# The start-up of a two-block attention kernel: how batch 0's rows arrive, what warms TensorE, and who normalises and rounds the rows

## The reference, cut to what matters

```
x = L0_attn_hidden_states                 # (2, 512, 256) f32: 2 batches of 512 tokens
xn = layernorm(x)                         # over the 256 features, eps 1e-5
s = attention0(xn, Wq, Wk, Wv, Wo)        # 16 heads, 4 key/value heads, head size 16
g = silu(ffn0(xn, w_gate_up, w_down))     # 256 -> 2 x 1024 -> 256
x = x + s * g
...                                       # second block: linear attention and
                                          # a mixture of 8 experts, top 1
```

## The kernel before, in words

Two places of the program that the steps below speak of:

```
            for b in range(B):
                dve.wait_ge(x_in_s[b], 16)
                norm_sums(TB * b, TB * b + TB)
                for stage in range(4):
                    norm_root(b, stage)
                apply_norm(0, b)
...
    fill[KD:5 * KD] = [*up0, *fill[2 * KD:3 * KD], *gate2, *fill[3 * KD:4 * KD]]
    early(KD)


    stacks = [("stack_T", 0, c) for c in STACK_ORDER]
    plan += stacks[:3]
```

## Time and profile before

| | us |
|---|---|
| median of three runs (lowest, highest) | 345.54 (345.40, 347.27) |
| the profiled execution | 345.08 |
| its span, first to last instruction | 343.3 |
| PE busy | 315.3 (92%) |
| DVE busy | 228.9 (67%) |
| ACT busy | 158.7 (46%) |
| POOL busy | 61.5 (18%) |

### The profile page before, as it was taken

The page is one execution under the profiler, slowest core; times in us unless marked ns, Lnnn a source line. Parts: engine busy times, 40 slices in busy tenths (PEclk is TensorE's granted clock), DMA queues, the critical chain, the costliest instruction groups (busy, mean ns, idle before and its releaser), DMA issues.

```text
span 343.3 us, 4810 instructions
## 1 busy us (share of the span) xinstructions
PE 315.3 (92%) x1602; PEld 186.8 (54%) x1602; DVE 228.9 (67%) x494; ACT 158.7 (46%) x289; POOL 61.5 (18%) x80
## 2 busy tenths in 40 slices
PE   2977989999999999999999999999989999999940
PEld 2645565454465454465545456556655676666630
DVE  3997848778475676877976763039898575446940
ACT  1476514575776655554474465523315622232310
POOL 5007750000010000000000002100503421033063
PEclk9999989999999999999999999999999999999995
DMA  7900019028091370400000006108934993038410
GB/s 250 406 6 2 0 49 201 1 61 191 1 207 45 83 169 1 124 0 3 1 1 3 0 1 207 41 2 326 361 95 118 392 428 140 30 124 258 165 53 20
DMA packets 19483, 39.19 MB, mean 114 GB/s; under 512 B 1826, under 2 KB 15363, under 8 KB 18176
## 3 DMA queue, kind: packets, MB, share of 16 engines
q1 hardware_dynamic: 17904, 35.69, 32.6%
q0 software_dynamic: 1552, 3.15, 2.6%
HBM read 34.54 MB, written 15.22 MB: 145 GB/s over the span
## 4 chain that ended last, share of the span: by engine, by line
PE 78%; DVE 15%; issue 3%; ACT 1%; DMA 1%; POOL 1%; DVEq 0%; POOLq 0%; ACTq 0%
PE ps L1728 12%; PE ps L1673 9%; PE ps L1641 8%; PE ps L1741 8%; PE ps L1663 7%; PE ps L1783 6%; PE ps L1799 6%; PE ps L1811 6%; PE ps L1546 3%; DVE nmax L1222 3%; PE ps L1580 2%; PE ps L1848 2%; PE ps L1525 2%; PE ps L1773 1%; DMA x<-in_x 1%
## 5 line engine op out<-in xcount | busy, mean ns | idle before, releaser
L1222 DVE TENSOR_REDUCE nmax<-ps 128x1 f32<-128x512 f32 x128 | 85.5, 687 | 35.0 <-PE ps L1641 34.3
L957 ACT ACTIVATE shared<-ps 128x512 f32<-128x512 f32 x128 | 74.1, 594 | 53.6 <-PE ps L1663 52.7
L1641 PE MATMUL ps<-experts 96*128 96x512 bf16 x128 | 48.2, 384 | 1.6 <-DVE experts L1229 1.1
L1663 PE MATMUL ps<-experts 99*128 99x512 bf16 x128 | 48.3, 382 | 0.0
L1741 PE MATMUL ps<-shared,experts 128*128 128x256 f32 x128 | 37.5, 386 | 0.0
L1673 PE MATMUL ps<-shared,experts 128*32 128x512 f32 x256 | 34.1, 605 | 0.3 <-ACT shared L957 0.3
L1641 PEld LDWEIGHTS ps<-experts 96*128 96x128 bf16 x128 | 12.5, 98 | 36.7 <-DVE nmax L1222 18.3
L1741 PEld LDWEIGHTS ps<-shared,experts 128*128 128x128 f32 x128 | 23.4, 190 | 8.9 <-issue 2.5
L965 ACT ACTIVATE experts<-ps 96x1024 bf16<-96x1024 bf16 x18 | 17.9, 1018 | 11.6 <-PE ps L1580 11.6
L1546 PE MATMUL ps<-late_weights,xnT 128*128 128x512 f32 (+1 forms) x64 | 22.5, 492 | 0.3 <-DVE shared L1134 0.3
L1783 PE MATMUL ps<-experts,shared 128*128 x88 | 20.9, 380 | 0.8 <-ACT shared L1032 0.8
(11 more groups left out here) (232 smaller groups left out, 516.9 us busy)
## 6 DMA issues: line engine op xcount, KB each, us to landing
experts<-in_experts SPq DMA_DIRECT2D x8, 1536.0 KB, 11.3
slot_rows<-in_empty SPq DMA_DIRECT2D x4, 2080.0 KB, 12.2
shared<-in_wgu SPq DMA_DIRECT2D x1, 2048.0 KB, 10.9
x<-in_x SPq DMA_DIRECT2D x2, 512.0 KB, 5.5
shared<-in_wdn SPq DMA_DIRECT2D x1, 1024.0 KB, 12.8
expert_results<-in_empty SPq DMA_DIRECT2D x1, 1024.0 KB, 6.9
token_rows<-x SPq DMA_DIRECT2D x1, 1024.0 KB, 16.0
token_rows<-gx SPq DMA_DIRECT2D x1, 1024.0 KB, 4.5
```

The source lines that it names most:

```text
L957: nc.scalar.activation(probs[:, n % 2, hh, :], ps[:, 2 + hh % 2, :], ACT.Exp, scale=float(HD) ** -0.5).then_inc(s["exp_done"], 1)
L1222: nc.vector.tensor_reduce(nmax[:, 4 * t + hh:4 * t + hh + 1], ps[:, m % 2, :], AX, ALU.max, negate=True).then_inc(s["max_done"], 1)
L1641: nc.tensor.matmul(ps[:, m % 2, :], qs[0:KS, b, GR * g + hh, P * t:P * t + P], ks[0:KS, b, g, :], start=True, stop=True).then_inc(s["score ...
L1663: nc.tensor.matmul(ps[:, 2 + hh % 2, :], ks[0:KM, b, g, P * t:P * t + P], qs[0:KM, b, GR * g + hh, :], start=True, stop=True).then_inc(s[" ...
```

## The change

- SP loads batch 0's rows in four transfers of 128 KB, each with a semaphore of its own, and DVE waits tile by tile in `norm_sums`. All later loads are issued behind them.
- DVE first writes 0.5 into a 128x128 part of `tanh_g` (`halves_ready`). PE starts its warm-up on that tile: 22 f32 products instead of 18 transposes, and it waits for the constants only afterwards.
- DVE normalises tiles 0 and 1 of batch 0, ACT tiles 2 and 3 (`half_norm`). The counts of `rows_norm` are adapted to that.
- ACT does `projections(0)` ahead of `round_rows(0, k)`.
- DVE computes `x_low` of batch 0 behind `prepare(0)` instead of ahead of it.
- In `plan` the first two gate pieces stand behind the first three stacks instead of ahead of them.

```diff
-WARM_UP = 18
+WARM_UP = 22
...
     fill[KD:5 * KD] = [*up0, *fill[2 * KD:3 * KD], *gate2, *fill[3 * KD:4 * KD]]
-    early(KD)
-
-
     stacks = [("stack_T", 0, c) for c in STACK_ORDER]
     plan += stacks[:3]
+    early(KD)
...
-            sp.dma_start(x[:, 0:TB, :], x_in[:, 0:TB, :]).then_inc(x_in_s[0], 16)
+            for j in range(TB):
+                sp.dma_start(x[:, j, :], x_in[:, j, :]).then_inc(x_in_s[j], 16)
             sp.dma_start(cst[:, 0:early_c], const_in[:, 0:early_c]).then_inc(s["const_loaded"], 16)
             sp.dma_start(wqkv, wqkv_in).then_inc(s["wqkv_loaded"], 16)
-            sp.dma_start(x[:, TB:NT, :], x_in[:, TB:NT, :]).then_inc(x_in_s[1], 16)
+            sp.dma_start(x[:, TB:NT, :], x_in[:, TB:NT, :]).then_inc(x_in_s[TB], 16)
...
             nc.scalar.activation(identb[:], ident, ACT.Copy).then_inc(s["identb_ready"], 1)
+            act.wait_ge(s["std_ready"], 1)
+            for j in range(TB // 2, TB):
+                nc.scalar.activation(xn[:, j, 0:D], x[:, j, :], ACT.Identity, scale=st1[:, 4, j:j + 1], bias=st1[:, 5, j:j + 1]
+                                     ).then_inc(s["half_norm"], 1)
...
             round_weights(0)
             round_weights(1)
+            projections(0)
             for k in range(KD):
                 round_rows(0, k)
-            projections(0)
...
-            def norm_sums(j0, j1):
+            def norm_sums(j0, j1, first=False):
 
                 for j in range(j0, j1):
+                    if first:
+                        dve.wait_ge(x_in_s[min(j, TB)], 16)
                     last = nc.vector.bn_stats(bn[:, j, :], x[:, j, :])
...
+            nc.vector.memset(tanh_g[:, 0, 0:P], 0.5).then_inc(s["halves_ready"], 1)
             for b in range(B):
-                dve.wait_ge(x_in_s[b], 16)
-                norm_sums(TB * b, TB * b + TB)
+                norm_sums(TB * b, TB * b + TB, first=True)
                 for stage in range(4):
                     norm_root(b, stage)
-                apply_norm(0, b)
+                apply_norm(0, b, TB if b else TB // 2)
...
-            dve.wait_ge(s["qkv_psum"], TB)
-            for k in range(KD):
-                dve.wait_ge(s["x_high_ready"], k + 1)
-                nc.vector.tensor_tensor(x_low(0, k), xnT[:, k, 0:S], x_high(0, k).bitcast(F32), ALU.subtract).then_inc(s["x_low_ready"], 1)
...
             nc.vector.tensor_copy(place_in_stack(5, 0, HEADS), place_in_stack(1, 0, HEADS)).then_inc(s["slots_copied"], 1)
+            dve.wait_ge(s["qkv_psum"], TB)
+            for k in range(KD):
+                dve.wait_ge(s["x_high_ready"], k + 1)
+                nc.vector.tensor_tensor(x_low(0, k), xnT[:, k, 0:S], x_high(0, k).bitcast(F32), ALU.subtract).then_inc(s["x_low_ready"], 1)
...
-            pe.wait_ge(s["const_loaded"], 16)
 
-            keep_warm(WARM_UP, 7)
+            pe.wait_ge(s["halves_ready"], 1)
+            for _ in range(WARM_UP):
+                nc.tensor.matmul(ps[:, 7, 0:P], tanh_g[:, 0, 0:P], tanh_g[:, 0, 0:P], start=True, stop=True)
+            pe.wait_ge(s["const_loaded"], 16)
             for b in range(B):
                 for t in range(TB):
-                    pe.wait_ge(s["rows_norm"], TB * b + t + 1)
+                    if b == 0 and t >= TB // 2:
+                        pe.wait_ge(s["half_norm"], t + 1 - TB // 2)
+                    else:
+                        pe.wait_ge(s["rows_norm"], t + 1 + TB // 2 * b)
```

More of the change, by code:

```diff
@@ L505, in two_gated_blocks @@
         miscb = misc.bitcast(BF16)
-        x_in_s = [sem(f"x_loaded{b}") for b in range(B)]
+        x_in_s = [sem(f"x_loaded{n}") for n in range(TB + 1)]
         names = ("raw_T raw_ready router_mean router_centred logits_scaled gates_ready acol_psum acol_ready act_step attn_T_ready bias_added branch_free branch_psum branch_ready "
-                 "const_loaded cos1 counts down_ready down_tanh dve_step e_down e_gate e_gated e_h e_tanh e_up "
+                 "const_loaded halves_ready half_norm cos1 counts down_ready down_tanh dve_step e_down e_gate e_gated e_h e_tanh e_up "
                  "early_gate_free early_up_free end_free exp_done experts_here first_part gate_free gate_ready heads_T "
@@ L803, in scatter @@
                 pool.wait_ge(s["slots_emptied"], 16 * EMPTYINGS)
-                pool.wait_ge(s["rows_norm"], NT + TB * (b + 1))
+                pool.wait_ge(s["rows_norm"], NT - TB // 2 + TB * (b + 1))
                 for j in range(TB * b, TB * b + TB):
@@ L1584, in _ @@
                     bank = place(it)[0]
-                    pe.wait_ge(s["rows_norm"], NT + TB * (b + 1))
+                    pe.wait_ge(s["rows_norm"], NT - TB // 2 + TB * (b + 1))
                     misc_bank(it)
```

## The result

The changed kernel took **348.07 us** (median of 4 runs, 347.34 to 348.78) against 345.47 for the kernel before in the same session (4 runs, 345.06 to 347.27): a ratio of **1.0089, 95% interval 1.0054 to 1.0123**, slower. Its profiled execution took 348.78 us, 3.7 more than the 345.08 of before. Forecast were 343.4 us and a range of 341.5 to 345.6. Both the time and the sign were missed.

A forecast was written before the change was run, and what follows sets the result against it. The DVE chain to the first score was taken as the bound, ACT's chain next. The score moving from 30.68 to 28.6 saves 2.1 us: 343.0 profiled, plus 0.46 for the median, 343.4; range 341.5 to 345.6.

The forecast's parts named there:

- Four transfers: Load of batch 0's rows: last quarter lands at 4.5, statistics end at 4.9 instead of 6.7, 1.8 us earlier.
- Half the normalising on ACT: Batch 0's normalising: DVE saves two of four tiles, 0.7 us, and the last tile is ready no later.
- Batch 1's rows: DVE comes to batch 1's rows at 8.4, they land at 8.8: a new wait of 0.4 us.
- Warm-up: PE's start: begins near 1.0, clock rises at 5.7, ends at 8.7; batch 0's transposes then take 1.04 us.
- ACT's new order: ACT and PE up to the first score: weights land at 13.6, batch 0's products end at 15.85, score at 28.6.
- the forecast's own list: Signs to check in the profile; weights landing after 14.4 was among those that would show the forecast wrong.
- DVE's new order: DVE before the first score: moved subtractions take 1.2, hidden by PE and ACT; uncovered they cost up to 1.2.
- Rival A: Longer PE wait before batch 1's products, 2.7 us, makes the clock fall once more: 344.9 us, chance 0.24.
- Rival C: Split loads delay the queue: rows at 5.8, weights at 14.4, first score at 29.2, total 344.0; chance 0.12.
- Rival D: PE's new warm-up leaves the clock low, so batch 0's products end at 21.5: 349 us, chance 0.10.

The follow-up runs named there:

- experiment 5: The changed kernel measured again, nothing altered: 348.94 us, ratio 1.0112 to the kernel before.
- experiment 7: experiment 1 with the old warm-up (18 transposes after the constants land): 345.81 us, ratio 1.0016 to the kernel before.
- experiment 9: experiment 1 with ACT copying batch 1's transposed rows before rounding batch 0's rows: 343.99 us, ratio 0.9953 to the kernel before.
- experiment 10: experiment 1 with DVE normalising all four tiles of batch 0: 346.46 us, ratio 1.0012 to the kernel before.
- experiment 14: The kernel before with the four transfers of batch 0's rows alone: 345.15 us, ratio 1.0020.
- experiment 1: The changed kernel, with POOL starting the low parts of weights 2 and 3 only after DVE's moved subtractions: 344.06 us, ratio 0.9991 to the kernel before.
- experiment 3: The kernel before with only the subtractions moved behind the preparation and the first gates behind the stacks: 348.09 us, ratio 1.0076.
- experiment 15: The changed kernel with batch 0's rows in one transfer again: 350.38 us, ratio 1.0150 to the kernel before.
- experiment 11: experiment 9 with 12 transposes before batch 1's products and 16 behind score 15: 343.77 us, ratio 0.9962 to the kernel before.
- experiment 6: experiment 1 with batch 0's rows in one transfer again: 345.96 us, ratio 1.0006 to the kernel before.
- experiment 4: experiment 3 with POOL also waiting for DVE's subtractions: 344.54 us, ratio 1.0010 to the kernel before.

## Why the prediction was wrong

By its steps:

- **Four transfers:** right in sign, mis-sized. Statistics of batch 0 end at 6.01 instead of 6.7, not at 4.9: a gain of 0.7 and not 1.8. The last piece took 5.58 - 2.12 = 3.5 from its issue, not half of 4.55; that half had no row behind it.
- **Half the normalising on ACT:** right. Both engines start at 8.83, ACT's two tiles take 1.09.
- **Batch 1's rows:** no wait came in this profile, since DVE was itself late, at 9.6. In five other profiles with four transfers (experiments 5, 7, 9, 10, 14) DVE waited 0.9 to 1.2 us for them, more than the 0.4 forecast.
- **Warm-up:** right. 44 records from 1.05 to 8.12 (8.7 forecast), and the eight transposes take 1.11. Busy time by stretch, line L1496 alone (PE with the number of records, PEld, clock, DMA share, GB/s):

```profile
4.00:5.00 1.00, 1.00 (x6) 1.00 (x6) 1.00 1.00 158
5.00:6.00 1.00, 1.00 (x11) 1.00 (x10) 1.00 0.67 231
```

From 6 records in a us to 11: the rise to 2.4 GHz is near 5.0 (5.7 forecast), while the clock's own column reads 1.00 on both sides of it. The forecast did well to go by the durations.
- **ACT's new order:** the weights were there at 14.73, not at 13.6. By the forecast's own list this is "wrong". Batch 1's products started at 20.25 instead of 19.6, 0.65 late, after a wait of 2.82 (2.7 forecast). The late weights are not what made them late: PE's products of batch 0 ended at 11.16 + 5.40 = 16.56, 0.7 behind the forecast's 15.85, and ACT could not have turned to their copies (16.64) before that. It is the first term, the four transfers, that comes back here.
- **DVE's new order: the step that failed.** "... so the moved subtractions are hidden by PE and ACT. If that cover goes, they cost up to 1.2." They cost 5.54 on the chain. The duration was taken from the place they came from the earlier trace rows, where POOL stood still, and carried to a place where POOL starts. That POOL waits for `parts_done` was known from the code; what starts there, on which inputs, and beside what it now runs was not asked. The forecast's "up to 1.2" was the full price of the two subtractions run alone, so the overlap that it had wrong was the one with POOL, not the one with PE and ACT. PE's stack transposes ended at 26.31 + 1.75 = 28.06; with the gates' 1.40 the score would have come at 29.46 (experiment 1: 29.93). So of the 4.5 us between forecast (28.6) and measured first score (33.14), 3.7 are this term (0.5 of them the low clock of the last three gate products, in the wake of the wait) and 0.9 the late chain ahead of it, and the low stretch behind adds 1.24.
- **Rival A:** half right. Two profiles of the changed kernel, one with the fall near 21 and one without; both have another fall at 32, behind the wait that exclusion made, which was nowhere in the forecast (experiment 3 has it too, at 33.5; experiment 15 does not).
- **Rival C:** right as a fact, and near in size: 14.73 passes its 14.4, and without the 3.7 the score would have come at 29.46 against its 29.2, though by late statistics more than by late weights. **Rival D**, the only one priced clearly slower, named a mechanism that did not occur; that its 349 lies near the 348.07 measured is luck. The chance of 0.09 for slower hung on the wrong story.

The large edits then moved the time little, even with exclusion taken away (experiment 1: 0.9991). Of the 2.1 forecast 0.75 is left at the first score of its profile. Its chain says where the rest went:

```profile
5.79 0.83 DVE bn L1093 x2
...
11.78 5.41 PE ps L1517 x16
...
17.21 1.30 ACT experts L900 x2
...
20.84 5.44 PE ps L1517 x16
```

The statistics end at 6.62 and not at 4.9, batch 0's products at 17.19 and not at 15.85, and that 1.3 stays to the end: 29.93 against 28.6. The weights (14.31) are not in this chain; in the profile of experiment 9 (15.95) they are. Where neither was late, in the profile of experiment 11 (statistics to 5.55, weights at 14.00), the first score came at 28.49, as forecast for the changed kernel, though with ACT's other order.

The second part is the gap before batch 1's products, which grew from 1.77 to 2.8 in the changed kernel. Of the seventeen profiles six have a wait of 1.77 there, and the products took 5.43 in each; ten have one of 2.6 to 4.0, and in eight of these a low stretch followed and they took 7.0 to 8.5. Such a fall costs more than the 0.75 gained. Experiment 9 takes ACT's rounding out of that gap and experiment 11, on top of it, fills it, and only these two beat the kernel before. That this is why they do is argued from their profiles and not shown apart: in experiment 9's own profile the gap was 2.59 and the fall came.

## What to carry to other kernels

A duration read at one place holds only beside the neighbours it had there: before moving a two-input DVE instruction, look at what POOL does at the new place and what releases it, and if POOL reads SBUF there, let the one that PE needs first go first, by a wait if need be. A last DVE step that signals POOL and then goes on with its own two-input work is a meeting by design. And an edit that shortens a chain by making PE wait longer in one piece should be booked with a fall of the clock as a likely cost (eight of the ten profiles with the longer wait before batch 1's products).

## What the hardware showed that was not expected

- One f32 subtraction of 128 x 512 on DVE takes 0.683 us alone, the same beside a POOL memset, and 2.845 beside a POOL subtraction of 128 x 1024; POOL's own goes from 2.35 to 2.81, and its next instruction from 1.53 to 1.98. DVE lost 4.3 us, POOL 0.9. A DVE copy from PSUM beside the same POOL subtraction keeps its 0.68.
- Four transfers of 128 KB gave DVE its first tile at 3.1 to 3.7 us and one of 512 KB at 5.1 to 5.4, but the 2 MB transfer issued behind the four was there up to 1.7 us later than the latest behind the one (15.95 against 14.21), being itself issued 1.4 us later.
- The low stretches of PE's clock before the last 20 us of each profile lasted 3.4 us or twice that (6.8, in experiments 3, 5, 6, 7, 10 and 15). Their places, near 11, 21, 33, 46 and 180 us, differ between profiles of one kernel and of kernels with the same waits; the profiles of experiments 1 and 4 have none before 329 us.
- Behind a wait of 1.77 us at the same place the clock never fell (six profiles), behind 2.6 to 4.0 it fell in eight of ten.
